# The last edge layer of a graph network on one core: 196 unrolled groups with seven slots, or a loop of 49 turns with four

## The reference

```python
weight = jnp.maximum(edge_rbf @ W1 + b1, 0.0) @ W2 + b2      # one filter of 128 per edge
h = x @ Wl + bl
msg = h[dst] * weight
out = jax.ops.segment_sum(msg, src, num_segments=6250)
x = layernorm(x + out)
```

## Time and profile before

| | us |
|---|---|
| median of 3 runs | 10863.49 |
| the runs | 10833.27 to 10908.15 |
| span of the profiled execution | 10911.3 |
| TensorE busy | 8137.0 (75%) |
| GpSimd busy | 5544.8 (51%) |
| VectorE busy | 4162.8 (38%) |
| ScalarE busy | 3246.9 (30%) |

### The profile page before, as it was taken

One profiled execution on the slowest core, in us unless ns is written; L12 is line 12 of the kernel. 1 busy time (PEld: TensorE's weight loads), 2 busy tenths in 40 slices (PEclk: granted clock), 3 DMA queues, 4 the chain that ended last, 5 costly groups with the idle time before them and its releaser, 6 DMA issues. The chain is left out here.

```text
span 10911.3 us, 154123 instructions
## 1 busy us (share of the span) xinstructions
PE 8137.0 (75%) x38400; PEld 4981.9 (46%) x38401; DVE 4162.8 (38%) x9898; ACT 3246.9 (30%) x5364; POOL 5544.8 (51%) x5296
## 2 busy tenths in 40 slices
PE   2988888888776666555688797887886777877776
PEld 1544444444435555555333343333334555555554
DVE  5887777643336666665400000000002222222223
ACT  3012345645556665555100000000002222222222
POOL 5888887777710000000355555555434655665664
PEclk7999999999995665666788898888987777877777
DMA  4234455656644333322566576666762222222222
GB/s 113 72 112 137 161 184 201 234 200 205 215 163 144 123 111 105 98 92 88 180 272 238 232 292 229 264 254 227 283 241 81 62 59 59 66 59 58 63 61 53
DMA packets 563180, 1661.60 MB, mean 152 GB/s; under 512 B 115313, under 2 KB 312029, under 8 KB 519494
## 3 DMA queue, kind: packets, MB, share of 16 engines
q1 hardware_dynamic: 324442, 1129.76, 28.3%
q0 software_dynamic: 206976, 473.99, 14.8%
q10 hardware_dynamic: 31536, 54.94, 1.4%
HBM read 1174.46 MB, written 483.82 MB: 152 GB/s over the span
## 5 line engine op out<-in xcount | busy, mean ns | idle before, releaser
L920 PE MATMUL wide<-ring 128*128 128x392 bf16 x14112 | 2519.8, 340 | 541.5 <-DVE ring L850 253.7
L527 POOL DMA_INDIRECT z_got<-z_table,z_idx x1568 | 2098.9, 1339 | 595.2 <-issue 468.7
L1546 POOL DMA_INDIRECT sorted_recs<-dn_rec_in,type_f x1568 | 1523.6, 972 | 1300.1 <-DMA dn_rec_in<-in_records 835.0
L1637 POOL DMA_INDIRECT l_rows<-h_table,l_recs x1568 | 1582.1, 1009 | 1176.0 <-DMA l_recs<-sorted_recs 725.3
L920 PEld LDWEIGHTS wide<-ring 128*128 128x128 bf16 x14112 | 1410.4, 100 | 1650.7 <-issue 900.1
L1405 PE MATMUL wide<-stream,X 128*128 128x512 f32 (+1 forms) x2548 | 1149.3, 602 | 255.2 <-issue 230.3
L1055 POOL DMA_DIRECT2D rows<-z_edges x196 | 103.5, 528 | 2055.9 <-PE wide L362 1849.1
L373 PE MATMUL wide<-rows,onehot 128*128 128x130 f32 x3904 | 858.1, 407 | 283.1 <-DVE A L390 283.1
L373 PE MATMUL wide<-l_rows,l_onehot 128*128 128x128 f32 x3904 | 669.5, 321 | 503.4 <-issue 326.7
L373 PEld LDWEIGHTS wide<-rows,onehot 128*128 128x128 f32 x3904 | 793.8, 310 | 341.4 <-DVE A L390 341.4
L1405 PEld LDWEIGHTS wide<-stream,X 128*128 128x128 f32 x2548 | 493.9, 201 | 876.7 <-issue 869.0
(11 more groups left out here) (260 smaller groups left out, 8430.1 us busy)
## 6 DMA issues: line engine op xcount, KB each, us to landing
stream<-w_dense SPq DMA_DIRECT2D x252, 1792.0 KB
stream<-c_dense SPq DMA_DIRECT2D x84, 1792.0 KB
z_edges<-z_got POOLq DMA_DIRECT2D x196, 528.0 KB
rows<-z_edges POOLq DMA_DIRECT2D x196, 528.0 KB
dst_bc<-in_dst_row SPq DMA_DIRECT2D x196, 512.0 KB
c_dense<-A SPq DMA_DIRECT2D x49, 1568.0 KB
w_dense<-A SPq DMA_DIRECT2D x49, 1568.0 KB
c_dense<-H SPq DMA_DIRECT2D x49, 1568.0 KB
```

The source lines that it names most:

```text
L527: e.indirect_dma_start(out=z_got[:, s, t, :], out_offset=None, in_=z_table, in_offset=bass.IndirectOffsetOnAxis(ap=z_idx[:, s, t:t + 1], a ...
L920: ins = e.matmul(banks[:, bass.ds(to[v], 1), int(m > 0), 0:WC].rearrange("p a x -> p (a x)"), lhsT=slots[:, k, m * P:(m + 1) * P], rhs=slo ...
L1546: e.indirect_dma_start(out=sorted_recs, out_offset=bass.IndirectOffsetOnAxis(ap=pos_i[:, g * TILES + t:g * TILES + t + 1], axis=0), in_=re ...
L1637: e.indirect_dma_start(out=rows[:, k, t, :], out_offset=None, in_=h_table, in_offset=bass.IndirectOffsetOnAxis(ap=recs[:, k, t, R_DST:R_DS ...
```

## The change

The last layer's programs become loops of 49 turns over four groups, on each of the five engines, and there are four slots in place of seven. TensorE and ScalarE run 48 turns in the loop, after a written-out start and before a written-out last turn. Thresholds of waits are worked out from the turn's number in a register. Each such wait, or two in a row, is followed by an increment of a semaphore that nobody waits for (`note`). The order of the steps on every engine, and the operations with their shapes, stay as they are.

```diff
@@ -58,7 +58,8 @@
 RW = N_RBF + 2
 R_DST, R_SRC = N_RBF, N_RBF + 1
 PLACE_AT = N_RELS
-REC_SLOTS, L3_SLOTS = 8, 7
+REC_SLOTS, L3_SLOTS = 8, 4
+L3_TURNS = NG // L3_SLOTS
 assert PLACE_AT + 2 * NB <= WIDE_TRIPS and NG % L3_SLOTS == 0
 assert TP * TC == NT and WP * WCOL == NW and KQ * NS == NB
 
@@ -1616,127 +1617,197 @@
...
-        def slot_of(g):
-            return g % L3_SLOTS, g // L3_SLOTS
+        def slot_rows(k):
+            return rows[:, k, :, :]
+
+        def in_turn(k, ahead):
+            return (k + ahead) % L3_SLOTS, (k + ahead) // L3_SLOTS
 
         with nc.Block() as block:
             @block.sync
             def _(e):
-                for g in range(NG):
-                    k, turn = slot_of(g)
-                    if turn:
-                        e.wait_ge(s_free, g - L3_SLOTS + 1)
-                    e.dma_start(recs[:, k, :, :], sorted_v[g, :, :, :]).then_inc(s_recs[k], 16)
+                for k in range(L3_SLOTS):
+                    e.dma_start(recs[:, k, :, :], sorted_v[k, :, :, :]).then_inc(s_recs[k], 16)
+                with e.Fori(1, L3_TURNS) as i:
+                    for k in range(L3_SLOTS):
+                        e.wait_ge(s_free, i * L3_SLOTS + (k + 1 - L3_SLOTS))
+                        e.sem_inc(note["sp"], 1)
+                        e.dma_start(recs[:, k, :, :], sorted_v[bass.ds(i * L3_SLOTS + k, 1), :, :, :].rearrange(
+                            "a p t w -> (a p) t w")).then_inc(s_recs[k], 16)
 
             @block.gpsimd
             def _(e):
-                for g in range(NG):
-                    k, turn = slot_of(g)
-                    e.wait_ge(s_recs[k], 16 * (turn + 1))
-                    for t in range(TILES):
-                        e.indirect_dma_start(
-                            out=rows[:, k, t, :], out_offset=None, in_=h_table,
-                            in_offset=bass.IndirectOffsetOnAxis(ap=recs[:, k, t, R_DST:R_DST + 1].bitcast(i32), axis=0)
-                        ).then_inc(s_got[k], 16)
+                with e.Fori(0, L3_TURNS) as i:
+                    for k in range(L3_SLOTS):
+                        e.wait_ge(s_recs[k], (i + 1) * 16)
+                        e.sem_inc(note["pool"], 1)
+                        for t in range(TILES):
+                            e.indirect_dma_start(
+                                out=rows[:, k, t, :], out_offset=None, in_=h_table,
+                                in_offset=bass.IndirectOffsetOnAxis(ap=recs[:, k, t, R_DST:R_DST + 1].bitcast(i32), axis=0)
+                            ).then_inc(s_got[k], 16)
                 for k in range(L3_SLOTS):
-                    e.wait_ge(s_got[k], 16 * TILES * len(range(k, NG, L3_SLOTS)))
+                    e.wait_ge(s_got[k], 16 * TILES * L3_TURNS)
 
...
-                def turn_attr(g):
-                    k, turn = slot_of(g)
-                    e.wait_ge(s_recs[k], 16 * (turn + 1))
-                    if g:
-                        e.wait_ge(s_attr, g)
+                def turn_attr(i, s):
+                    k, later = in_turn(s, 3)
+                    e.wait_ge(s_recs[k], (i + (later + 1)) * 16)
+                    e.wait_ge(s_attr, i * L3_SLOTS + (s + 3))
+                    e.sem_inc(note["pe"], 1)
+                    turn_slot(k)
+
+                def turn_slot(k):
...
+                def hide(i, s):
+                    e.wait_ge(s_attr, i * L3_SLOTS + (s + 3))
+                    e.wait_ge(s_hid, i * L3_SLOTS + (s + 2))
+                    e.sem_inc(note["pe"], 1)
+                    hide_half(s % 2)
+
...
+                def apply_filters(i, s):
+                    e.wait_ge(s_filt, i * L3_SLOTS + (s + 1))
+                    e.sem_inc(note["pe"], 1)
+                    begin_filters()
+                    e.wait_ge(s_hid, i * L3_SLOTS + (s + 2))
+                    e.sem_inc(note["pe"], 1)
+                    end_filters((s + 1) % 2)
+
+                def sums(i, s):
+                    lo, hi = block_range(e, table_src, i * L3_SLOTS + s, regs)
+                    e.wait_ge(s_msg, i * L3_SLOTS + (s + 2))
+                    e.sem_inc(note["pe"], 1)
+                    pe_sums(e, lo, hi, half_ready, half_done, slot_rows(s), F, c)
                     e.matmul(bank[3][0:1, 0:1], lhsT=one_col[:, 0:1], rhs=one_col[:, 0:1], start=True, stop=True
                              ).then_inc(s_free, 1)
 
-                for g in range(-3, NG):
-                    if g + 3 < NG:
-                        turn_attr(g + 3)
-                    if 0 <= g + 2 < NG:
-                        hide(g + 2)
-                    if 0 <= g + 1 < NG:
-                        apply_filters(g + 1)
-                    if g >= 0:
-                        sums(g)
...
+                with e.Fori(0, L3_TURNS - 1) as i:
+                    for s in range(L3_SLOTS):
+                        turn_attr(i, s)
+                        hide(i, s)
+                        apply_filters(i, s)
+                        sums(i, s)
...
+                def evict_attr(i, s):
+                    e.wait_ge(s_turn, i * L3_SLOTS + (s + 4))
+                    e.wait_ge(s_mm1, i * L3_SLOTS + (s + 2))
+                    e.sem_inc(note["act"], 1)
+                    copy_attr((s + 3) % 2)
...
-                for g in range(NG):
-                    k, turn = slot_of(g)
-                    lo, hi = block_range(e, table_src, g, regs)
-                    e.wait_ge(s_recs[k], 16 * (turn + 1))
-                    e.tensor_copy(src_f[:, g % 2, :], recs[:, k, :, R_SRC].bitcast(i32))
-                    e.drain()
-                    e.wait_ge(s_filt, g + 1)
-                    e.wait_ge(s_got[k], 16 * TILES * (turn + 1))
-                    e.tensor_tensor(rows[:, k, :, :], filters[:, g % 2, :].rearrange("p (t f) -> p t f", f=F),
-                                    rows[:, k, :, :], ALU.mult).then_inc(s_msg, 1)
-                    dve_sums(e, lo, hi, half_ready, half_done,
-                             lambda h: src_f[:, g % 2, 4 * h:4 * h + 4].unsqueeze(2), c, last_b, F)
+                e.sem_inc(s_msg, 1)
+                with e.Fori(0, L3_TURNS) as i:
+                    for k in range(L3_SLOTS):
+                        lo, hi = block_range(e, table_src, i * L3_SLOTS + k, regs)
+                        e.wait_ge(s_recs[k], (i + 1) * 16)
+                        e.sem_inc(note["dve"], 1)
+                        e.tensor_copy(src_f[:, k % 2, :], recs[:, k, :, R_SRC].bitcast(i32))
+                        e.drain()
+                        e.wait_ge(s_filt, i * L3_SLOTS + (k + 1))
+                        e.wait_ge(s_got[k], (i + 1) * (16 * TILES))
+                        e.sem_inc(note["dve"], 1)
+                        e.tensor_tensor(slot_rows(k), filters[:, k % 2, :].rearrange("p (t f) -> p t f", f=F),
+                                        slot_rows(k), ALU.mult).then_inc(s_msg, 1)
+                        dve_sums(e, lo, hi, half_ready, half_done,
+                                 lambda h: src_f[:, k % 2, 4 * h:4 * h + 4].unsqueeze(2), c, last_b, F)
```

More of the change, by code:

```diff
@@ L1696, in _ @@
+                last = L3_TURNS - 1
+                for s in range(L3_SLOTS):
+                    if s + 3 < L3_SLOTS:
+                        turn_attr(last, s)
+                    if s + 2 < L3_SLOTS:
+                        hide(last, s)
+                    if s + 1 < L3_SLOTS:
+                        apply_filters(last, s)
+                    sums(last, s)
             @block.scalar
             def _(e):
-                def evict_attr(g):
-                    e.wait_ge(s_turn, g + 1)
-                    if g >= 2:
-                        e.wait_ge(s_mm1, g - 1)
-                    e.copy(attr_t[:, g % 2, :], turned[0:N_RBF, :]).then_inc(s_attr, 1)
@@ L1716, in _, with copy_attr, copy_hidden @@
-                for g in range(-3, NG):
-                    if g + 3 < NG:
-                        evict_attr(g + 3)
-                    if 0 <= g + 2 < NG:
-                        evict_hidden(g + 2)
-                    if 0 <= g + 1 < NG:
-                        evict_filters(g + 1)
+                def copy_attr(a):
+                    e.copy(attr_t[:, a, :], turned[0:N_RBF, :]).then_inc(s_attr, 1)
+                def copy_hidden(a):
+                    e.activation(hid[:, a, :], hidden[:, :], ACT.Relu, bias=b1_col[:, 0:1]).then_inc(s_hid, 1)
@@ new lines, in _ @@
+                copy_attr(0)
+                e.wait_ge(s_mm1, 2)
+                copy_hidden(1)
+                e.wait_ge(s_mm2, 1)
+                copy_filters(0)
+                with e.Fori(0, L3_TURNS - 1) as i:
+                    for s in range(L3_SLOTS):
+                        evict_attr(i, s)
+                        evict_hidden(i, s)
+                        evict_filters(i, s)
+                last = L3_TURNS - 1
+                for s in range(L3_SLOTS):
+                    if s + 3 < L3_SLOTS:
+                        evict_attr(last, s)
+                    if s + 2 < L3_SLOTS:
```

(3 more changed lines are left out.)

61 lines of the change are left out of this document (37 added, 24 removed).

## The result

The changed kernel takes 11,428 us (median of 4 runs, 11,417 to 11,474) where the kernel before takes 10,878 us on the same chip (4 runs, 10,833 to 10,908): ratio 1.051, 95% interval 1.048 to 1.054. The forecast was 10,815 us, its range ended at 11,240. The change is 5% slower, outside the range.

A forecast was written before the change was run, and what follows sets the result against it. No engine full; the last layer's 13.06 us step held 8.06 us of work and 5 us of holds. Load and lower clock would replace the holds: 195 x (13.06 - 13.06) - 50 = -50 us, so 10,815 us; range 10,590 to 11,240.

The forecast's parts named there:

- the clock: TensorE's granted clock in the last layer: taken as 0.82 from its busy share, giving a step of 13.06 us.
- the better end: Of the granted clocks 0.79 to 0.82 in the last layer, 0.82 was taken, the new pause being short and regular.
- holds: Waits in the last layer for nothing the profile shows, 5 us a step; blamed on streamed code, the loop removing them.
- rival 3: Last layer's clock falls as in the first layer: 11,140 us at 0.70, 11,390 at 0.63; chance 0.13.
- The graph-building stage: A loop with GpSimd gathering and unbroken matmuls, 128 in 23.44 us; taken as evidence that holds go with streamed code.
- Rival 2: Holds stay, belonging to indirect DMAs and f32 matmuls; load comes on top: 11,180 to 11,490 us; chance 0.19.
- The load: With four slots SP's record load stands whole on TensorE's path: 3.07 us, 3.23 us a step with the mark.
- The 0.97 us: In a clean last-layer step with two pairs, the second pair's wait for VectorE, in one step of four.
- The start: Last layer's first load to first mark: 78.8 us held, 28 us expected without holds, saving 50 us.
- The back edge: Branch at the end of each of 49 loop turns: 0.21 us on TensorE, costed at nothing, at most 10 us.
- Rival 4: Each of 49 turns' back edges stalls 3.07 us for a fetch: 150 us more, 10,965 us; chance 0.03.

The follow-up runs named there:

- e8: Changed kernel with three added filler matmuls after the transposes, the pause left empty, on a chip with holds: 11,436 us, ratio 1.053.
- e15: Kernel before, one plain DMA a group in place of eight indirect ones (gather by node left out), on a chip with holds: 9,844 us, ratio 0.907.
- e3: Changed kernel with three added filler matmuls in the pause before each step's transposes, on a chip without holds: 9,757 us, ratio 1.020.
- e10: Changed kernel with the attributes turned later, behind the hidden layer and filters, on a chip with holds: 11,003 us, ratio 1.013.
- e18: Kernel before, unrolled, with four slots in place of seven and nothing else, on a chip with holds: 11,354 us, ratio 1.038.
- e1: Changed kernel's loop with seven slots, 14 turns of 14 groups, on a chip without holds: 9,565 us, ratio 0.9999.
- e4: Changed kernel with the record load let go earlier, at VectorE's multiply, on a chip without holds: 9,547 us, ratio 0.998.
- e5: The changed kernel itself, run on a chip without holds: 10,309 us, ratio 1.078 to the kernel before.
- e9: Changed kernel with one added filler matmul in the pause, on a chip with holds: 11,458 us, ratio 1.055.
- e14: Changed kernel with the record load's address written out, not computed (right records left out), on a chip without holds: 10,250 us, ratio 1.074.
- e2: Kernel before, unrolled, with four slots in place of seven and nothing else, on a chip without holds: 10,045 us, ratio 1.049.

## Why the prediction was wrong

**The step that failed is the clock.** "At clock c the step is 3.23 + 8.06/c", with c = 0.82. That c came from another sentence, "the granted level goes with the busy share", and this is what broke: at the same 75% the clock was 0.79 before and 0.70 after, and at 76% it is 0.86 in e8. Work at the half clock keeps TensorE busy for nearly twice as long (3.78 us against 1.98 for the first product in the rows above), so the share does not show it. The form has a flaw of its own: it needs the clock of the work, and rows 2 give means over work and idle time. With the 0.70 of the window after it gives 14.74 us and not 16.10, as the pauses themselves stand at the high clock (1.00 in the rows above, with 0.57 behind). The work at the full clock is, by e15, 1513.1 + 48.0 in 195 steps: 8.01 us. The measured 16.10 us is, each term a window's sum over 195: 7.76 of work, 4.35 for the half clock (2362.1 - 1513.1), 3.51 of pause, 0.48 for VectorE. The forecast had 8.06 (with 0.24 for VectorE in it), 1.77 and 3.23. Of the 3.04 us between 13.06 and 16.10, 2.58 are the clock term, 0.28 the pause, 0.23 VectorE's wait, and -0.05 the work. As c, 8.06 us became near 12.6: 0.64, the first layer's level. I took the better end since today's pauses are long and the new one is short and regular. It was the wrong way round: on this chip a pause in every step cost more clock than today's holds. e3 shows, on a chip without holds, that the clock is a cost of its own, 552 us gained by filling the pause. That was rival 3, at its far end (11,390 us for c = 0.63), with a chance of 0.13. The Trainium skill ("TensorE: Matmul & The Clock Gate", section "HAM oscillation") tells of a kernel that waits for a transfer in every tile and starts every tile at the low clock. The trace agrees in kind, not for every step: behind 187 of the 192 pauses at least part of the work ran at the low level, behind 5 none did.

**The holds: right in effect by luck, wrong in cause.** No idle time of TensorE's matmuls by "issue" is left after the change, and ScalarE's attribute copy comes within a microsecond of the transposes in the step shown, as forecast. But not because of the loop: e10 has holds in a loop without instruction packets, e15 none in streamed code, and e18, unrolled, loses the idle time by "issue" as well. The four slots did it, by the pause that they put before every step. The graph-building stage, on which I leaned, has bf16 matmuls, and beside the same indirect DMAs it is within 2% the same on both kinds of chip; it was no clean contrast. What remains of the holds are late signals: the mean pause is longer than on a chip without holds (3.51 against 3.11 us a step), as 42 of 192 are over 4 us here and none there. Rival 2, holds by indirect DMAs and f32 matmuls, named what the runs bear out, and a right time, 11,180 to 11,490 us, but not the way: what it had stay beside the load did not, and its 3.23 us on top of 13.06 was a sum of other terms.

**The load was right, but for the late ones.** Once in a step, released by the record load, 3.07 and 3.06 us in the rows against 3.07; 3.51 as a mean on this chip. The 0.97 us that a second pair "waits for VectorE" are by "issue" in rows 4; e15 bears the reading out, with 48.0 us in 49 waits for VectorE.

**The start** saved 28 us, not 50: the first mark comes 51.0 us after the first load, before 78.8.

**The back edge** costs nothing that shows (e1, ratio 0.9999, 14 turns; e4, 0.998, 49), and the packets of the instruction queue go, as forecast. Rival 4 is out. The loop is not free with four slots: 0.41 us more of pause, of which the address is 0.06.

**Open.** What a hold is, why three chips of the six have none, and why a pause in every step takes away the idle time by "issue". The filled pause (e3) was never run on a chip with holds, so what the clock alone would give back there is not shown. Why the low clock costs 4.35 us a step on the chip of the result and (2115.1 - 1513.1) / 195 = 3.09 on one without holds: the late loads of the first have a part in it, for behind none of its 42 pauses over 4 us did the work run at the full clock; but behind the 147 pauses of 2.9 to 3.4 us it did so 5 times, and in e5 behind 18 of 186, and that is not explained. Which instruction of the loop delays SyncE.

## What to carry to other kernels

Count slots against the program order of the engine that frees and needs them: when the load for the next use is allowed by the instruction just before the one that waits for it, its whole latency stands on the path, and the low clock behind the pause can cost as much again. Give the load another trigger (e4) or put other work between before taking slots away. And when a trace of before shows idle time that nothing ends, find out by an experiment what it belongs to before booking it as a gain; a contrast of two stages that differ in two things settles nothing. Do not read the clock to come from a busy share, as the low clock raises the share.

## What the runs showed of the hardware

- Two kinds of chips differ by about 14% on the same program: 9,554 to 9,569 us on three, 10,867 to 10,935 on three others, each in one comparison. The dense stage moves 338 GB/s on one kind and 256 on the other.
- Where there are holds, TensorE's signals arrive late (4.8 us in e9, 10.7 us in e10) and its unwaited instructions stand still (296.7 us by "issue" in the sums' matmuls from first to last mark), in a stage of f32 matmuls beside GpSimd's indirect DMAs. Where a pause opens each step no such idle time is left, in a loop or unrolled (after, e18). One plain DMA a group in place of eight indirect ones gave steps of 8.01 us, against 13.06. A stage of bf16 matmuls beside indirect DMAs was within 2% the same on both kinds.
- Without holds the clock cost of a pause, as busy time over e15's 1513.1 us by 195: 3.09 us a step with a mean pause of 3.11 us (e5), 2.70 us with 3.05 (e14), 2.31 us with 2.70 (e2, none longer than 3.3), nothing with 0.58 (e3: 2055.3 us busy less 542.9 of its added matmuls is 1512.4).
- The granted clock can differ at one busy share of TensorE: 0.70, 0.79, 0.86 at 75 to 76% (after, before, e8).
